# Regrouping the last batch's four row tiles from two and two into three and one

## The reference

```
# 1. gated delta rule (8 heads, 128 x 128 state each), a scan over 512 tokens per batch, then an MLP
S = S * a_t;  S = S + k_t (v_t - k_t S) b_t;  o_t = q_t S
h = (rms_norm(o) * o_norm_w * silu(h Wg)) Wo;   x1 = x + h
y = square(relu(rms_norm(x1) W_fc)) W_proj;     x = layernorm(x + x1 + y)
# 2. attention of each token over 8 given rows of the context (softmax per head), x = layernorm(x + attn)
# 3. mixture of experts: 8 experts, top 2, capacity 320 rows each, positions by a running count over all
#    tokens in order; gelu(x w1 + b1) w2 + b2 weighted by the gates, x = layernorm(x + moe)
```

## Time and profile before

| what | us |
|---|---|
| median of three runs | 704.04 (699.05 to 709.57) |
| the profiled execution | 709.15 |
| its span, first to last instruction | 707.1 |
| mean granted TensorE clock | 0.940 of full |
| steps 5, 6, 7 of the last batch and its `between`, to the last scatter issued | about 562 to 628 |

### The profile page before, as it was taken

One profiled execution on the slowest core, in us unless ns is written; L12 is line 12 of the kernel. 1 busy time (PEld: TensorE's weight loads), 2 busy tenths in 40 slices (PEclk: granted clock), 3 DMA queues, 4 the chain that ended last, 5 costly groups with the idle time before them and its releaser, 6 DMA issues.

```text
span 707.1 us, 15060 instructions
## 1 busy us (share of the span) xinstructions
PE 601.8 (85%) x5466; PEld 493.6 (70%) x5466; DVE 475.1 (67%) x1846; ACT 422.3 (60%) x807; POOL 300.6 (43%) x263
## 2 busy tenths in 40 slices
PE   2848988998999889899988899999899997779940
PEld 1446777787788778687777788887788884437730
DVE  4787934688788577878875678869547874623314
ACT  2734546998756499796654899866245744114413
POOL 3035002446434536645604455376214352236753
PEclk9968989999999999999999999999889999999985
DMA  8703150012102301120041011300500440023253
GB/s 253 274 1 61 43 117 2 31 32 53 38 18 81 64 23 46 38 60 20 30 107 39 18 44 46 69 22 27 106 3 1 165 126 3 17 53 51 23 97 103
DMA packets 82321, 42.50 MB, mean 60 GB/s; under 512 B 50448, under 2 KB 74457, under 8 KB 81864
## 3 DMA queue, kind: packets, MB, share of 16 engines
q1 hardware_dynamic: 78280, 39.34, 20.8%
q0 software_dynamic: 3968, 2.20, 2.4%
HBM read 28.43 MB, written 14.46 MB: 61 GB/s over the span
## 4 chain that ended last, share of the span: by engine, by line
PE 38%; DVE 20%; ACT 17%; issue 11%; POOL 8%; DMA 5%; SPq 0%; ACTq 0%; POOLq 0%; DVEq 0%
PE ps L759 8%; PE ps L724 3%; DVE blk_t L1987 3%; PE ps L1339 3%; DVE prod L1980 3%; PE ps L1329 3%; DVE uo L1846 3%; ACT L1393 2%; PE ps L807 2%; PE ps L1134 2%; ACT L1417 2%; ACT att L1417 2%; PE ps L1219 2%; PE ps L1002 2%; PE ps L989 2%
## 5 line engine op out<-in xcount | busy, mean ns | idle before, releaser
L532 POOL TENSOR_TENSOR att<-att,br 128x512 f32<-128x512 f32 x32 | 33.3, 1046 | 120.5 <-ACT att L1417 89.6
L518 POOL TENSOR_TENSOR st<-st,mhalf 128x4 f32<-128x4 f32 (+1 forms) x23 | 21.7, 945 | 126.4 <-DVE st L2096 83.5
L518 POOL TENSOR_TENSOR of<-oss,mhalf 128x4 f32<-128x4 f32 x32 | 32.8, 1025 | 68.7 <-DVE oss L1883 68.7
L1987 DVE TENSOR_TENSOR blk_t<-blk_t,prod 128x126 f32<-128x126 f32 (+35 forms) x244 | 52.0, 252 | 0.1
L759 PEld LDWEIGHTS ps<-kT 128*128 128x128 f32 x256 | 35.7, 209 | 20.1 <-issue 18.5
L1980 DVE TENSOR_TENSOR prod<-kn,blk_t 128x126 f32<-128x126 f32 (+35 forms) x244 | 49.4, 241 | 0.3 <-DMA kn<-n_blocks 0.3
L759 PE MATMUL ps<-qT,kT 128*128 128x128 f32 x256 | 41.4, 314 | 6.6 <-DVE att L1888 5.3
L527 POOL TENSOR_TENSOR att<-att,const 128x512 f32<-128x512 f32 x24 | 30.5, 1269 | 38.7 <-DMA att<-y_rows 38.7
L1846 DVE SCALAR_TENSOR_TENSOR uo<-uo,of,gate_sb 128x128 f32<-128x128 f32 x128 | 44.0, 405 | 4.3 <-POOL of L518 4.2
L759 PE MATMUL ps<-kT 128*128 128x128 f32 x256 | 37.6, 296 | 9.6 <-DVE Nm L1831 9.0
L1013 PEld LDWEIGHTS ps<-ones,kT 128*128 128x128 f32 x256 | 33.0, 195 | 12.5 <-issue 11.8
(11 more groups left out here) (261 smaller groups left out, 1754.7 us busy)
## 6 DMA issues: line engine op xcount, KB each, us to landing
att<-y_rows SPq DMA_DIRECT2D x24, 256.0 KB, 3.3
att<-y_rows SPq DMA_DIRECT2D x2, 1024.0 KB, 5.3
tt_blocks<-gate_sb SPq DMA_DIRECT2D x4, 512.0 KB, 3.3
TT<-tt_blocks SPq DMA_DIRECT2D x16, 128.0 KB, 2.6
Nm<-in_L_ffn_w SPq DMA_DIRECT2D x1, 2048.0 KB, 9.3
kn<-in_L_ffn_w SPq DMA_DIRECT2D x8, 256.0 KB, 4.7
n_blocks<-Nm SPq DMA_DIRECT2D x16, 96.0 KB, 3.2
kn<-n_blocks SPq DMA_DIRECT2D x4, 384.0 KB, 3.3
```

The costliest lines, as they stand in the source:

```text
L518: pool.tensor_tensor(out_ap, in_ap, mhalf[:, 0:n], ALU.pow).then_inc(done, 1)
L532: pool.tensor_tensor(heads(att[:, slot(kb, m)]), heads(att[:, slot(kb, m)]), bc(br[:, kb % 2, unit(m)].unsqueeze(2), [P, HG, P]), ALU.mult ...
L1987: last = tt(rows_t, rows_t, pr, ALU.subtract)
```

## The change

FIRST becomes row tiles 0 to 2, LAST row tile 3 alone. Since row tile 2 is projected in step 6, FIRST's ladder begins in step 7 instead of step 5. FIRST's buffers are resized, and the orders on all four engines are rewritten:

```diff
-        parts += [(B - 1, 0, 2, KT, EB, EB), (B - 1, 2, CH, HP, OT, OT)]
+        parts += [(B - 1, 0, 3, KT, EB, EB), (B - 1, 3, CH, HP, OT, OT)]
...
 # GpSimd, step(b, s)
-                if b == B - 1 and s == 5:
+                if b == B - 1 and s == 7:
                     post_r1(FIRST)
                 elif b == B - 1 and s == 6:
-                    count_bias(FIRST)
                     post_scatter(b - 1, 0)
                     post_scatter(b - 1, 1)
...
                 if b == B - 1 and s == 6:
                     post_scatter(b - 1, 2)
+                    post_scatter(b - 1, 3)
                 elif b == B - 1 and s == 7:
-                    post_rs1(FIRST)
+                    count_bias(FIRST)
 # GpSimd, between(b)
-                    post_scatter(b - 1, 3)
+                    post_rs1(FIRST)
                     post_r1(LAST)
-                    post_rs2(FIRST)
                     count_bias(LAST)
                     post_rs1(LAST)
+                    post_rs2(FIRST)
                     post_rs2(LAST)
 # TensorE, step(b, s): behind scan_au
                 if kb >= B and s == 7:
-                    post_y(FIRST)
-                if kb >= B and s == 6:
+                    post_mT(FIRST)
                     post_fc(FIRST, 0)
                     post_fc(FIRST, 1)
...
-                if kb >= B and s == 6:
+                if kb >= B and s == 7:
                     post_fc(FIRST, 2)
                     post_fc(FIRST, 3)
 # TensorE, between(b)
                     out_transpose(b, NU - 1)
-                    keep_busy(4)
+                    post_y(FIRST)
+                    out_proj(b, NU - 1)
+                    keep_busy(3)
                     post_aT(FIRST)
-                    out_proj(b, NU - 1)
-                    post_sc(FIRST)
-                    keep_busy(6)
                     post_mT(LAST)
                     post_fc(LAST, 0)
                     post_fc(LAST, 1)
-                    post_pT(FIRST)
+                    post_sc(FIRST)
                     post_fc(LAST, 2)
                     post_fc(LAST, 3)
-                    post_xo(FIRST)
                     post_y(LAST)
                     keep_busy(3)
+                    post_pT(FIRST)
+                    post_aT(LAST)
+                    post_xo(FIRST)
+                    post_sc(LAST)
+                    keep_busy(4)
+                    post_pT(LAST)
                     post_x2T(FIRST)
+                    post_xo(LAST)
                     post_lg(FIRST)
                     keep_busy(4)
-                    post_aT(LAST)
-                    post_sc(LAST)
+                    post_x2T(LAST)
+                    post_lg(LAST)
                     keep_busy(4)
                     post_cum(FIRST)
-                    keep_busy(4)
-                    post_pT(LAST)
-                    post_xo(LAST)
-                    keep_busy(10)
-                    post_x2T(LAST)
-                    post_lg(LAST)
-                    keep_busy(10)
+                    keep_busy(8)
                     post_cum(LAST)
 # ScalarE, between(b)
                     out_T(b, NU - 1)
                     post_aT(FIRST)
-                    post_sexp(FIRST)
                     post_mT(LAST)
                     post_relu2(LAST, 0)
                     post_relu2(LAST, 1)
-                    post_pT(FIRST)
+                    post_sexp(FIRST)
                     post_relu2(LAST, 2)
                     post_relu2(LAST, 3)
+                    post_pT(FIRST)
+                    post_aT(LAST)
+                    post_sexp(LAST)
+                    post_pT(LAST)
                     post_x2T(FIRST)
...
 # VectorE, step(b, s): ahead of out_sum, and behind it
-                if kb >= B and s == 5:
+                if kb >= B and s == 7:
                     post_x1(FIRST)
                     post_ssx(FIRST)
...
                     out_sum(b, s)
+                    if kb >= B and s == 7:
+                        post_m(FIRST)
 # VectorE, between(b)
                     gate_out(b, NU - 1)
-                    post_a(FIRST)
+                    post_a_stats(FIRST)
                     post_x1(LAST)
                     post_ssx(LAST)
+                    post_a(FIRST)
+                    post_m(LAST)
                     post_scores(FIRST)
-                    post_m(LAST)
+                    post_a_stats(LAST)
                     post_probs(FIRST)
+                    post_a(LAST)
                     post_x2_stats(FIRST)
+                    post_scores(LAST)
                     post_x2(FIRST)
-                    post_a_stats(LAST)
+                    post_probs(LAST)
                     post_logits(FIRST)
-                    post_a(LAST)
+                    post_x2_stats(LAST)
                     post_choice(FIRST)
-                    post_scores(LAST)
-                    post_probs(LAST)
+                    post_x2(LAST)
                     post_places(FIRST)
                     post_slots(FIRST)
-                    post_x2_stats(LAST)
-                    post_x2(LAST)
                     post_logits(LAST)
```

More of the change, by code:

```diff
@@ L328, in x2_of @@
             if q == FIRST:
-                return xh[:, :, :].rearrange("p c n -> p (c n)")[:, 0:2 * ROW].rearrange("p (c n) -> p c n", c=2)
+                return xh[:, :, :].rearrange("p c n -> p (c n)")[:, 0:3 * ROW].rearrange("p (c n) -> p c n", c=3)
             return x2_rows[:, parts[q][1]:parts[q][2]]
@@ L333, in fT @@
             if q == FIRST:
-                return att[:, 2 + f // 2, (f % 2) * 2 * P:(f % 2 + 1) * 2 * P]
+                return att[:, 2 + f, 0:3 * P]
             if q == LAST:
-                return kT[:, 2 + f // 2, (f % 2) * 2 * P:(f % 2 + 1) * 2 * P]
+                return kT[:, 2, f * P:(f + 1) * P]
             return att[:, slot(q, NU - 2 + f)] if f < 2 else ogT[:, f - 2]
@@ L977, in post_piece @@
                     post_lg(b - 1)
-                elif s == 6 and b == B - 1:
-                    post_mT(FIRST)
             def q_proj(kb, n):
@@ L1268, in post_cum @@
                     pe.wait_ge(sm["lsub_ok"], q + 1)
-                mm(bank[:, span(q, E, 64)], le, mask, start=True, stop=False, skip_group_check=True)
+                last = mm(bank[:, span(q, E, 64)], le, mask, start=True, stop=(n == 1), skip_group_check=True)
                 for i in range(1, n):
@@ L1529, in between @@
                     post_relu2(LAST, 1)
-                    post_pT(FIRST)
+                    post_sexp(FIRST)
                     post_relu2(LAST, 2)
                     post_relu2(LAST, 3)
+                    post_pT(FIRST)
+                    post_aT(LAST)
+                    post_sexp(LAST)
+                    post_pT(LAST)
                     post_x2T(FIRST)
-                    post_aT(LAST)
                     post_lexp(FIRST)
-                    for stage in (post_sexp, post_pT, post_x2T, post_lexp):
-                        stage(LAST)
+                    post_x2T(LAST)
+                    post_lexp(LAST)
                     return
@@ L1930, in step @@
                     elif s == 5:
-                        post_m(FIRST)
                         post_places(b - 1)
                         post_slots(b - 1)
-                    elif s == 7:
-                        post_a_stats(FIRST)
                 if key and m - 1 < NU and not last_key:
```

## The result

The changed kernel is slower: 721.8 us in the median of four runs (720.13 to 723.72), against 705.9 for the kernel before beside it. A ratio here is taken over the faster executions only, those within 1.5% of the shortest of their kernel (709.57 us of before falls out), and lies above the quotient of the two medians, 1.0225. On the 704.04 us of the forecast 1.0272 is 723.2 us, or +19.2 with an interval of +15.8 to +22.5, where +13.0 and at most 722 were forecast. The profiled execution took 722.63 us.

A forecast was written before the change was run, and what follows sets the result against it. The issue of the last GpSimd scatter was taken as the bound: +10.7 us at full clock plus 2.3 for the clock gave +13.0 on 704.04, or 717.0 us; range +5 to +18, 709 to 722.

The forecast's parts named there:

- The front: Last scan steps, up to FIRST's statistics: FIRST's power waits behind four scatters, delaying unit 7's transposes; 6.3 us, 1.3 gain counted.
- The blocked probabilities: VectorE in the tail: FIRST's probabilities wait behind LAST's statistics, which need LAST's y; some 3 us.
- the tail: From FIRST's statistics to the last scatter's issue; forecast from 598.8 to 638.6 us at full clock.
- The queue of eight: GpSimd at the end: all eight scatters of batch 3 queue behind FIRST's indices; 9.8 us, last at 638.6.
- the edits at nothing: Cum flags, moved count_bias(FIRST), x2 stores; experts wait as before, TensorE perhaps idle 3 us, up to 1.7 us if clock falls.
- LAST's indices after 636: Sign of a wrong forecast: then a chain, not GpSimd's scatter queue, sets the end; they were forecast at about 633.
- The table load: ScalarE's load for Exp, now between LAST's Relu and FIRST's Exp; 0 on the path, or 1.2 us with a drain.
- The clock: TensorE gaps lower the granted clock, mainly behind 600 us; between 0 and 4.8 us, half taken, +2.3.
- Rival 2: Half clock all through the tail and into the first expert; +15 to +18, 720.5 us; chance 0.2.
- The clock that stays up (1): Fillers and the denser first part keep TensorE at 2.4 GHz; +7 to +11, 713 us at +9; chance 0.2.
- FIRST's indices six scatters ahead of LAST's (3): Faster: the wait for m is covered, GpSimd's queue is empty, LAST's shorter chain sets the end; 698.7 us; chance 0.03.
- That little is lost (4): FIRST's transposes find m at once, but the queue of eight scatters remains; +2 to +6, 708 us; chance 0.07.

The follow-up runs named there:

- all four edits: Changed kernel with FIRST's power before four scatters, unit 7 before FIRST's first layer, FIRST's probabilities before LAST's y, and fitted fillers; ratio 1.0058 against before.
- kernel with fillers: Changed kernel with 68 more TensorE products that nothing reads, ahead of FIRST's transposes in step 7 and in the tail's gaps; ratio 1.0114 against before.
- probabilities first: Changed kernel with FIRST's probabilities ahead of LAST's statistics on VectorE, and their transposes ahead of LAST's y on TensorE; ratio 1.0178 against before.
- unit 7 first: Changed kernel with unit 6's projection and unit 7's gate ahead of FIRST's transposes and first layer in step 7; ratio 1.0157 against before.

## Why the prediction was right and where it was wrong

The direction, the places and the order of the terms were right; the sum was too small, and the time lay above the range.

**The front** was forecast at +6.3 us on unit 7's transposes, from 588.94 to 595.3, and measured at 30.54 - 23.86 = +6.7 within the stretch. FIRST's power, forecast 18.9 into the stretch, came at 18.63; post_m 19.8 and 19.56; gate_out(7) 29.0 and 28.82; FIRST's statistics 33.7 and 34.04. The wait of TensorE for m was 6.72 us for "7". Moving the power (2.4 us) and moving unit 7 (2.9) showed both parts of it as causes, and the clock is 1.5 more. Of the 12.7 us by which FIRST's statistics come later, all four edits leave 7.4, which no run takes apart.

**The blocked probabilities** were priced at some 3 us and gave 3.3 of the tail (2.6 against the second trace of the changed kernel).

**The queue of eight** came as told: 9.8 us from FIRST's indices to the last scatter, 640.91 - 631.08 = 9.83, LAST's indices ready 5.2 us earlier. Without three of them it is LAST's ladder that ends the stretch. What I overlooked is that the last scatter is not yet the experts: the 32 fillers, which I had filed under the edits at nothing with "some 3 us" of idle time behind them, end only 0.5 us before the rows are there.

**LAST's indices after 636** was one of my signs of being wrong. They were ready at 635.71 in a trace whose stretch begins 3.0 us earlier, so at 638.7 on the forecast's scale, and FIRST's at 634.1 for 628.8. Both slipped by more than 5 us together, and so the queue, not a chain, still set the last scatter.

**The table load** stood between LAST's Relu and FIRST's Exp. It ended at 604.74, the scores were ready at 605.42 and Exp began at 605.45, so it cost nothing; no run tells what it would cost there on the path. The 0.71 us from load to Exp is waiting for the scores, and no drain shows, as in the earlier trace rows.

**The clock is the step that failed:** the term "I take half of it, +2.3". At full clock I had put the tail at 638.6 - 598.8 = 39.8 us. The kernel with fillers shows 40.01 at a clock of 0.91: that sum was about right. For the clock I wrote that between 0 and 4.8 us were to be had and "I take half of it, +2.3", since my gaps lay between those of the rows at half and at full. Measured is 44.78, which is +5.0 (+4.3 in the second trace): about the whole of the upper end. Rival 2 (half clock all through the tail, chance 0.2) was in the main the case that came, at a clock of 0.58. Its extra for the first expert did not come here: TensorE reached the experts at full clock, after fillers and 0.5 us of idle time, and experts and final sums took 74.8 us (720.6 - 645.82) against 74.0 (707.1 - 633.08). It did come in the trace of "probabilities first", where the rest took 3.5 us more. Half of the price, between two extremes, was a guess that no row stood for. In the five traces that keep this order of the tail its clock was 0.58 to 0.69, and none came near the 42.1 us that +2.3 stands for: the four with eight scatters took 43.5 to 44.8.

**What the baseline hides.** The forecast of +13.0 stands against +15.95 in the pair of traces; the clock is 2.7 of these 3 us. The other 3.2 us up to +19.2 are not in the change. The first trace of before had a tail of 41.54 us and the second of 39.34, so the stretch's excess is 15.2 to 18.1 us over the four pairings of two traces each, 16.7 between their means. That is 2.4% of 706 us, inside both intervals (2.24 to 3.2% and 2.1 to 3.0%). I had carried +13.0 over from the profiled execution as if its own luck were the median's. The two medians of the first measurement differ by 15.9 us too (721.8 - 705.9), 2.3%. That the first ratio's middle lies at 2.72% is within its interval; part of it is which executions it is taken over, and how much stays open.

**The rivals.** The clock that stays up (1) was false. FIRST's indices six scatters ahead of LAST's (3) was off by far: they were 4.6 us ahead and the queue needs 7.7. Even with the power ahead of the scatters and the three other edits the stretch is 3.5 to 5.7 us longer than before's. That little is lost (4) was false too: the transposes of FIRST did not find m at once but waited 6.72 us for it.

## What to carry to other kernels

Before moving a step in a hand-written order, list what then stands ahead of it on each in-order engine, the DMA issues on GpSimd above all: here four scatters stood ahead of one power and cost 2.4 us. A step that waits belongs behind what is ready, even when the step is the more urgent one: unit 7 waited 8 us behind a step that was not ready, and 2.9 of them counted. Ask of a filler what stands behind it, too: 32 of them at the end hide most of what a shorter queue would give. When a schedule opens gaps on TensorE, price the rest of the stretch at the low clock until a trace shows otherwise; 68 fillers took 6.3 us back from the stretch, each single reordering 3.2 to 3.7.

## What the runs showed of the hardware that was not expected

The granted clock in the changed kernel's tail was 0.50 (1.2 GHz) from 614 to 640 us, though TensorE was never idle for more than 2.6 us in it and was busy for most of 626 to 632. What it did there was fillers, products of 8 columns and transposes, at half speed. Of the kernel before, a wait of 2.67 us was followed by half clock only from about 588.5 to 591.8; it fell again in parts of 612 to 616 and 622 to 626. I can't say from these traces what it would have taken to bring the clock up sooner; the fillers did.

Identical code ahead of the change ended between 558.00 us (all four edits) and 571.24 (unit 7 first). The first two traces, at 565.08 and 562.09, differ in where the low clock fell between 500 and 524 us. The 25 executions of the kernel before that were taken beside later runs spread from 701.34 to 716.77 us.
